# A second expert bias added on TensorE from a resident table, in place of a broadcast transfer a tile

## The chip, the cores and the metric

The kernel runs on one core of one Trainium2 chip. The metric is the device time of one execution in microseconds (us); a lower time is better. The engines are TensorE (PE in the rows; its weight loads are PEld), VectorE (DVE), ScalarE (ACT), GpSimd (POOL) and SyncE (SP), which here only issues transfers. Each engine has an instruction stream of its own and waits on semaphores for the others.

## The reference, cut to what matters

128 images are cut into 64 patches each, projected to 128 numbers (with a class token that makes T = 65 tokens), multiplied by a position table, passed through an LSTM over the tokens, and then through a mixture of 16 experts of which each token uses two. The change is in the last line of the expert step:

```
tokens = einsum('bpi,hi->bph', patches, W) + b ; h = [cls, tokens] * pos_embed
h = h + lstm(layernorm(h))                    # gates = x W_ih' + h W_hh' + biases, 65 steps
xt = layernorm(h)
topk_p, topk_i = top_k(softmax(xt @ router_w.T + router_b), 2)
for each expert e:
    hid = gelu(xt @ w1[e].T + b1[e])           # 128 -> 512
    y   = hid @ w2[e].T + b2[e]                # 512 -> 128, b2[e] is a row of 128
    out += y * gate[e]
h = h + out
```

## The kernel before

There are two stages. In the first, `step(n)` is one time step of the LSTM for all 128 images; beside it the same slot projects the patches of a later token, splits a piece of the expert weights into two fp16 parts, and routes and sends finished tokens to a buffer in HBM that is sorted by expert. In the second, `step_b(n)` works on tiles of 256 sorted rows that belong to one expert each. There are 80 tiles (TILES_B). The order is written out by hand: `slots(step, step_b)` walks both loops for every engine, and each engine executes its part of slot n in the order of the code.

A product of two fp32 matrices is made of three fp16 matmuls (high by high, low by high, high by low), with the weights scaled by E_SCALE = 256. In slot n of the second stage the engines do this:

- **SP** loads the rows of tile n + 3 (`xt`, line L532), after it has waited for `in_ps` and `dst_done` of tile n - 1 (L405). It then waits for `y_done` of tile n - 3, reads the expert number of tile n + 1 into a register (L540) and starts the transfer that spreads row b2[e] over 128 partitions (`b2r`, L542). Loads and stores of finished tokens come behind it in some slots.
- **PE** transposes tile n + 1 (2 fp32 passes, L1408), multiplies tile n by the first weight (12 matmuls over 256 columns, L1434) and tile n - 2 by the second (24 matmuls over 128 columns, L1452). Its waits: `in_done` of an earlier tile before the transposes, `hlo_done` of tile n - 2 ahead of L1434 and again of L1452, and `y_done` of the tile whose PSUM bank is used again.
- **ACT** applies gelu to the four quarters of tile n (L680), then rounds all of it to fp16 (`round_off`, L689). In slots from 54 on it also scales one or two rows of a finished chunk (L669).
- **DVE** casts the input of tile n + 1 (L1107), makes the result `yo` of tile n - 3 out of PSUM (L1114, the line that is changed: result times 1/256 plus `b2r`), makes the low part of the input (L1121), the low part of the hidden layer of tile n - 1 (`remainder`, L1099) and the destination rows (L1132). In slots from 56 on it also adds finished chunks (L1172, L1183).
- **POOL** scatters the two halves of tile n - 3 to HBM (`back`, L1257).

The buffers of the second stage lie in `arena`, the space that `patches` used in the first. Expert numbers of the tiles are read from the table `tabi`.

Of the kernel before, what the change touches and what calls it, by code (L numbers as in the profile page):

```python
# [47 lines left out]
PIECES = E * 2 * FF // PIECE  # L48
TWICE = 16
# [29 lines left out]
C_ID, C_TRI, C_ONE, C_IOTA, C_EBASE, C_TOK, C_BSC, C_POW, C_J = np.cumsum([0, P, P, P, UG * E, E, T, 4, 1]).tolist()  # L79
C_END = C_J + 1  # L80


def constants():

    c = np.zeros((P, C_END), np.float32)
    c[:, C_ID:C_TRI] = np.eye(P)
    c[:, C_TRI:C_ONE] = np.triu(np.ones((P, P)), 1)
    c[:, C_ONE:C_IOTA] = 1.0
    c[:, C_IOTA:C_EBASE] = np.tile(np.arange(E) - E, UG)
    c[:, C_EBASE:C_TOK] = np.arange(E) * CAP  # L90
    c[:, C_TOK:C_BSC] = 2 * (T * np.arange(P)[:, None] + np.arange(T))
    c[:, C_POW] = -0.5
    c[:, C_BSC:C_POW] = [0.5, 0.5, 1.0, 0.5]
    c[:, C_J] = ROWS * np.arange(P)
    return c


def tower(nc, x, w, w_rest, cls, pos, w_ih, w_hh, b_ih, b_hh, rw, rb, we, b1, b2, const, out):
# [3 lines left out]
    with ctx:  # L102
# [71 lines left out]
        h1 = sb("h1", [P, T, HID])  # L174
        ynT = sb("ynT", [HID, 2, B])
# [33 lines left out]
        pad = sb("pad", [P, HALVES, ROW])  # L209

# [14 lines left out]
        b2r = part(4 * HID).rearrange("p (a h) -> p a h", a=4)  # L225
# [77 lines left out]
        b2_in = [sem(f"b2_in{i}") for i in range(4)]  # L303
# [138 lines left out]
        def _(sp):  # L442
            at_row, at_expert, at_pad = (sp.alloc_register(name) for name in ("at_row", "at_expert", "at_pad"))
# [19 lines left out]
            def step(n):  # L463
# [22 lines left out]
                for piece in pieces_of(n + 2):  # L486
                    if piece >= NE:
                        through(sp, ex_lo_done, piece - NE)
                    sp.dma_start(ex_raw[:, piece % NE, :], we[:, bass.ds(piece * PIECE, PIECE)]
                                 ).then_inc(ex_in[piece % NE], 16)  # L490
                if n == 10:
                    sp.wait_ge(setup_dve, 2)
                    sp.dma_start(rows_of(sent, E * CAP), pad[:, :, :]).then_inc(pads, 16)
# [20 lines left out]
            def step_b(n):  # L514
# [18 lines left out]
                j = n + 1  # L533
                if 0 <= j <= TILES_B - 1:
                    if j == 0:
                        sp.wait_ge(tok_done, (T - 1))
                        sp.wait_ge(lo_done, (T - 1))
                    if j >= 4:
                        through(sp, y_done, j - 4)
                    sp.reg_load(at_expert, tabi[0:1, 0, j:j + 1])  # L540
                    e = sp.snap(at_expert, min_val=0, max_val=E - 1)
                    sp.dma_start(b2r[:, j % 4, :],  # L542
                                 b2[bass.ds(e, 1), :].rearrange("a h -> (a h)").partition_broadcast(P)
                                 ).then_inc(b2_in[j % 4], 16)
# [22 lines left out]
        def _(act):  # L567
# [30 lines left out]
            def step(n):  # L598
# [43 lines left out]
                if 0 <= t <= T - 1:  # L642
# [3 lines left out]
                    act.activation(xT_hi[:, t % 2, :], ps_T[:, 0:P], ACT.Copy).then_inc(xT_hi_done, 1)  # L646
                for p in pieces_of(n):
# [66 lines left out]
        def _(dve):  # L714
# [41 lines left out]
            def step(n):  # L756
# [90 lines left out]
                if n > T - 1:  # L847
                    routing(n)
                    rest_of_choice(n)
                if n == PLAN_B:  # L850
# [155 lines left out]
            def plan_piece(k, late):  # L1006
# [8 lines left out]
                start = cst[:, C_J:C_END]  # L1015
# [85 lines left out]
            def step_b(n):  # L1101
# [7 lines left out]
                if 0 <= j <= TILES_B - 1:  # L1109
                    through(dve, down_ps, j)  # L1110
                    dve.wait_ge(b2_in[j % 4], (j // 4 + 1) * 16)
                    if j >= NO:
                        dve.wait_ge(y_out[j % NO], j // NO * 16 * HALVES)
                    dve.scalar_tensor_tensor(yo[j % NO], ps_down(j).rearrange("p (a h) -> p a h", a=HALVES),  # L1114
                                             1.0 / E_SCALE,
                                             b2r[:, j % 4, :].unsqueeze(1).to_broadcast([P, HALVES, HID]), ALU.mult,
                                             ALU.add).then_inc(y_done, 1)
# [146 lines left out]
        def _(pe):  # L1264
# [131 lines left out]
            def step_b(n):  # L1396
# [41 lines left out]
                if 0 <= j <= TILES_B - 1:  # L1438
# [5 lines left out]
                    elif j > 0:  # L1444
                        through(pe, h1_done, T - 1)
                        through(pe, yT_done, T - 1)
                    for c in range(FC):
                        for k, (h_, w_) in enumerate(((hhi, ex_hi), (hlo, ex_hi), (hhi, ex_lo))):
                            w2 = w_[:, bass.ds(e, 1), 1, c * HID:(c + 1) * HID].rearrange("p a f -> p (a f)")
                            for a in range(HALVES):  # L1450
                                h = h_[j % 4][:, c * ROWS + a * P:c * ROWS + (a + 1) * P]
                                last = pe.matmul(ps_down(j)[:, a * HID:(a + 1) * HID], h, w2,  # L1452
                                                 start=(c == 0 and k == 0 and a == 0), stop=(c == FC - 1 and k == 2),
# [47 lines left out]
```

## Time and profile before

| | |
|---|---|
| time, median of 3 runs | 675.24 us (674.0 to 675.88) |
| span of the profiled execution | 771.4 us |
| the profiled execution's own time | not listed apart from its span |
| mean granted TensorE clock | 0.957 of 2.4 GHz |
| busy time PE / DVE / ACT / POOL | 647.2 / 562.3 / 493.0 / 413.1 us |
| first stage (65 LSTM steps) | from 0 to about 410 us of the span |
| tiles: first and last result (L1114) | 426.2 and 753.1 us, 80 of them |

The span runs from the first to the last instruction while every instruction is recorded. The timed runs are made without a recording, and here they are 96 us shorter than the span. A busy share is thus a share of a stretched time, and the time of single instructions and the distance of two that follow each other at once are better guides than shares. A busy matmul time includes the time to drain, during which the next already runs.

### The profile page before, as it was taken

What the parts mean: (1) busy time and instruction counts of PE and PEld (TensorE: products, weight loads), DVE (VectorE), ACT (ScalarE), POOL (GpSimd) and SP (SyncE); (2) the same over time, 40 slices, a digit from 0 to 9 for tenths busy, and PEclk for the clock granted to TensorE, in tenths of its full rate; (3) what the DMA queues carried; (4) which work ended last, traced back from release to release, by engine and by line L of the source; (5) the groups of instructions that cost most, each with busy time, mean ns of one, the idle gap of its engine ahead of it and who ended that gap; (6) DMA issues with size and microseconds to landing.
All of it is one profiled execution on the core that took longest, in us unless ns stands there. A gap on an engine that the chain in (4) does not pass through costs nothing.

```text
span 771.4 us, 24553 instructions
## 1 busy us (share of the span) xinstructions
PE 647.2 (84%) x7952; PEld 594.7 (77%) x7952; DVE 562.3 (73%) x1797; ACT 493.0 (64%) x1259; POOL 413.1 (54%) x446
## 2 busy tenths in 40 slices
PE   4999999999999999988877665878888787888870
PEld 4999999999999999888875554766666666666660
DVE  3877888888888888778886444756565756677777
ACT  4678876766667666554446343657666767777783
POOL 0243344777767666655656646545555555545552
PEclk9999999999999999999997767999999999999995
DMA  8987877888888887765522222344323234444555
GB/s 318 372 263 271 277 253 251 261 267 256 276 261 267 276 244 236 236 213 182 162 64 60 71 63 73 108 123 119 111 78 98 78 93 118 138 137 131 170 177 195
DMA packets 71895, 141.67 MB, mean 184 GB/s; under 512 B 13078, under 2 KB 55650, under 8 KB 63838
## 3 DMA queue, kind: packets, MB, share of 16 engines
q1 hardware_dynamic: 62128, 121.69, 50.1%
q0 software_dynamic: 9280, 17.21, 6.4%
q8 instruction: 70, 1.15, 0.6%
q10 hardware_dynamic: 366, 1.21, 0.5%
q14 instruction: 51, 0.42, 0.2%
HBM read 116.35 MB, written 25.66 MB: 184 GB/s over the span
## 4 chain that ended last, share of the span: by engine, by line
PE 25%; DVE 24%; another core or an unknown queue 13%; issue 13%; ACT 4%; POOL 3%; DMA 1%; POOLq 0%; ACTq 0%; DVEq 0%; SPq 0%
PE pair L1279 14%; DVE patches L1099 7%; PE pair L1434 3%; DVE patches L1121 2%; PE pair L1325 2%; POOL sent L1235 2%; ACT pair L680 2%; PE pair L1452 2%; PE pair L1289 1%; DVE patches L1114 1%; DVE h L1172 1%; DVE patches L1107 1%; DVE patches L1132 1%; DVE field L843 1%
## 5 line engine op out<-in xcount | busy, mean ns | idle before, releaser
L1257 POOL DMA_INDIRECT back<-patches x160 | 157.0, 981 | 150.6 <-DVE patches L1114 104.6
L680 ACT ACTIVATE pair<-pair,b1s 128x256 f32<-128x256 f32 x320 | 126.3, 448 | 110.4 <-remote 51.5
L1279 PE MATMUL pair<-field,patches 128*128 128x128 f32 (+1 forms) x1408 | 173.9, 280 | 8.9 <-DMA patches<-in_x 8.6
L1279 PEld LDWEIGHTS pair<-field,patches 128*128 128x128 f32 (+1 forms) x1408 | 164.6, 194 | 9.6 <-issue 8.6
L1235 POOL DMA_INDIRECT sent<-pay,slot_own x130 | 149.2, 1148 | 40.3 <-issue 38.2
L1434 PE MATMUL pair<-patches,ex_hi 128*128 128x256 f16 x640 | 119.4, 280 | 47.8 <-DVE patches L1099 23.8
L605 ACT ACTIVATE gate<-pair,lbias 128x128 f32<-128x128 f32 x260 | 74.4, 369 | 98.1 <-PE pair L1294 88.6
L1452 PE MATMUL pair<-ex_hi,patches 128*128 x1280 | 117.4, 225 | 8.3 <-issue 6.1
L1247 POOL TENSOR_TENSOR rstd<-veps,cst 128x2 f32<-128x2 f32 (+1 forms) x68 | 58.0, 853 | 107.2 <-DVE veps L800 106.6
L1107 DVE CAST patches<-pair 128x256 f16<-128x256 f32 x80 | 33.7, 422 | 109.6 <-remote 105.2
L1434 PEld LDWEIGHTS pair<-patches,ex_hi 128*128 x640 | 56.6, 99 | 72.8 <-issue 64.0
L1099 DVE TENSOR_TENSOR patches<-pair,patches 128x1024 f16<-128x1024 f32 x80 | 97.5, 1219 | 5.6 <-ACT patches L689 4.7
L1434 PE MATMUL pair<-patches,ex_lo 128*128 128x256 f16 x320 | 89.2, 279 | 13.6 <-issue 13.5
L1452 PEld LDWEIGHTS pair<-ex_hi,patches 128*128 128x128 f16 x1280 | 90.1, 101 | 13.5 <-issue 9.7
L1279 PE MATMUL pair<-field 128*128 128x128 f16 x1536 | 96.1, 219 | 0.0
L1279 PEld LDWEIGHTS pair<-field 128*128 128x128 f16 x1536 | 91.8, 98 | 0.8
L1452 PE MATMUL pair<-ex_lo,patches 128*128 x640 | 90.8, 225 | 0.0
L587 ACT ACTIVATE field<-patches 128x512 f16<-128x512 f32 x128 | 80.9, 634 | 4.6 <-DMA patches<-in_x 4.6
L689 ACT ACTIVATE patches<-pair 128x1024 f16<-128x1024 f32 x80 | 82.0, 1025 | 2.5
L843 DVE TENSOR_TENSOR field<-patches,field 128x1024 f16<-128x1024 f32 x64 | 78.1, 1221 | 0.1
L1209 POOL TENSOR_TENSOR ex_lo<-field,ex_hi 128x256 f16<-128x256 f32 x64 | 45.5, 720 | 43.3 <-ACT field L653 42.6
L1434 PEld LDWEIGHTS pair<-patches,ex_lo 128*128 x320 | 31.9, 100 | 28.0 <-issue 23.6
(150 smaller groups left out, 1257.7 us busy)
## 6 DMA issues: line engine op xcount, KB each, us to landing
patches<-in_x SPq DMA_DIRECT2D x62, 1152.0 KB
patches<-sent SPq DMA_DIRECT2D x80, 130.0 KB
field<-in_we SPq DMA_DIRECT2D x64, 128.0 KB
field<-back SPq DMA_DIRECT2D x10, 768.0 KB
patches<-in_b SPq DMA_DIRECT2D x80, 64.0 KB
field<-in_pos SPq DMA_DIRECT2D x65, 64.0 KB
out_tower<-h SPq DMA_DIRECT2D x10, 384.0 KB
back<-patches POOLq DMA_INDIRECT x160
```

The lines of the kernel that those rows point to most:

```text
L587: return act.activation(xhi[r][:, a:b, :], xraw[q][:, a:b, :], ACT.Copy)
L605: last = act.activation(gate[:, GATE_AT[g], :], ps_gate[n % 2][:, g * B:(g + 1) * B], ACT.Tanh, bias=lbias[:, 2, g:g + 1], scale=(1.0 if g ...
L680: last = act.activation(up[:, cols], up[:, cols], ACT.Gelu, bias=b1s[:, bass.ds(e * FC + 2 * half + i, 1)], scale=1.0 / E_SCALE)
L689: act.activation(hhi[n % 4], pair[n % 2][:, :], ACT.Copy).then_inc(hhi_done, 1)
L843: dve.tensor_tensor(xlo[r][:, :, :], xraw[q][:, 0:KS, :], xhi[r][:, :, :], ALU.subtract).then_inc(lo_done, 1)
L1099: dve.tensor_tensor(hlo[n % 4], pair[n % 2][:, :], hhi[n % 4], ALU.subtract).then_inc(hlo_done, 1)
L1235: pool.indirect_dma_start(sent, bass.IndirectOffsetOnAxis(ap=slot_own[:, g % 4, choice, col:col + 1], axis=0), pay[:, t % NP, :], None, bo ...
L1247: pool.tensor_tensor(rstd[:, both], veps[:, both], cst[:, C_POW:C_POW + 1].to_broadcast([P, both.stop - both.start]), ALU.pow).then_inc(rs ...
L1257: pool.indirect_dma_start(back, bass.IndirectOffsetOnAxis(ap=dsti[j % NO][:, k:k + 1], axis=0), yo[j % NO][:, k, :], None, bounds_check=2 ...
L1279: last = pe.matmul(bank_of, l, w_, start=(c == KS and k == 0), stop=(c == KS - 1 and k == 2))
L1434: last = pe.matmul(ps_up(n, half)[:, i * ROWS:(i + 1) * ROWS], w1, r, start=(k == 0), stop=(k == 2))
L1452: last = pe.matmul(ps_down(j)[:, a * HID:(a + 1) * HID], h, w2, start=(c == 0 and k == 0 and a == 0), stop=(c == FC - 1 and k == 2), skip_ ...
```

## The change

The table of 16 second biases is loaded once, twice over (partitions 0 to 15 and 16 to 31), in slot 0 of the first stage. ACT multiplies it by 256 in slot 4; DVE in slot 5 rounds it to fp16 (`b2_hi`) and forms `b2_parts`: partitions 0 to 15 hold the scaled table rounded to fp16, partitions 16 to 31 hold what the rounding left. The sum of row e and row 16 + e is the bias to about twice the precision of fp16. `chosen` holds two 16 by 16 unit matrices, one above the other. For every tile PE takes column e of it, repeated 128 times, as the stationary operand (32 rows by 128 columns) and `b2_parts` as the moving one, once for each half of the tile. These two matmuls open the accumulation in PSUM that the 24 of L1452 opened before. DVE's L1114 loses its second tensor and becomes a multiplication by a constant. SP loses the register load, the transfer and the wait for `y_done`. The constants `cst` grow by 17 columns. In the diff the name ahead of the point tells the engine (`sp`, `act`, `dve`, `pe`).

```diff
+BIASES_AT = 4
...
+    c[E:2 * E, C_PART] = -1.0
+    c[0:2 * E, C_SEL:] = np.tile(np.eye(E), (2, 1))
...
+        b2_raw = h1[0:2 * E, T - 1, :]
+        b2_hi = h1[0:2 * E, T - 2, 0:HID // 2].bitcast(F16)
...
+        b2_parts = sb("b2_parts", [2 * E, HID], F16)
+        chosen = sb("chosen", [2 * E, E], F16)
...
-        b2r = part(4 * HID).rearrange("p (a h) -> p a h", a=4)
...
+                if n == 0:
+                    for k in range(2):
+                        sp.dma_start(b2_raw[k * E:(k + 1) * E, :], b2).then_inc(b2_in, 16)
...
-                j = n + 1
-                if 0 <= j <= TILES_B - 1:
-                    if j == 0:
-                        sp.wait_ge(tok_done, (T - 1))
-                        sp.wait_ge(lo_done, (T - 1))
-                    if j >= 4:
-                        through(sp, y_done, j - 4)
-                    sp.reg_load(at_expert, tabi[0:1, 0, j:j + 1])
-                    e = sp.snap(at_expert, min_val=0, max_val=E - 1)
-                    sp.dma_start(b2r[:, j % 4, :],
-                                 b2[bass.ds(e, 1), :].rearrange("a h -> (a h)").partition_broadcast(P)
-                                 ).then_inc(b2_in[j % 4], 16)
...
+                if n == BIASES_AT:
+                    act.wait_ge(b2_in, 32)
+                    act.activation(b2_raw, b2_raw, ACT.Copy, scale=E_SCALE).then_inc(b2_scaled, 1)
...
+                if n == BIASES_AT + 1:
+                    dve.wait_ge(b2_scaled, 1)
+                    dve.tensor_copy(b2_hi, b2_raw).then_inc(b2_rounded, 1)
+                    dve.tensor_copy(chosen[:, :], cst[0:2 * E, C_SEL:C_END])
+                    dve.wait_ge(b2_rounded, 1)
+                    dve.scalar_tensor_tensor(b2_parts[:, :], b2_hi, cst[0:2 * E, C_PART:C_PART + 1],
+                                             b2_raw, ALU.mult, ALU.add).then_inc(b2_done, 1)
...
                     through(dve, down_ps, j)
-                    dve.wait_ge(b2_in[j % 4], (j // 4 + 1) * 16)
...
-                    dve.scalar_tensor_tensor(yo[j % NO], ps_down(j).rearrange("p (a h) -> p a h", a=HALVES),
-                                             1.0 / E_SCALE,
-                                             b2r[:, j % 4, :].unsqueeze(1).to_broadcast([P, HALVES, HID]), ALU.mult,
-                                             ALU.add).then_inc(y_done, 1)
+                    dve.tensor_scalar(yo[j % NO], ps_down(j).rearrange("p (a h) -> p a h", a=HALVES), 1.0 / E_SCALE,
+                                      None, ALU.mult).then_inc(y_done, 1)
...
+                    if j == 0:
+                        pe.wait_ge(b2_done, 1)
+                    one = chosen[:, bass.ds(e, 1)].to_broadcast([2 * E, P])
+                    for a in range(HALVES):
+                        pe.matmul(ps_down(j)[:, a * HID:(a + 1) * HID], one, b2_parts[:, :], start=(a == 0),
+                                  stop=False, skip_group_check=True)
                     for c in range(FC):
...
-                                                 start=(c == 0 and k == 0 and a == 0), stop=(c == FC - 1 and k == 2),
+                                                 start=False, stop=(c == FC - 1 and k == 2),
```

PE's instructions of one tile in the middle of the second stage, from the end of the first weight's matmuls to the next tile's transposes, before (ISA and REGISTER_ALU compute addresses from the expert number in a register):

```order
L1434 MATMUL pair<-patches,ex_lo 128x256
L1452 ISA [waits y_done,hlo_done]
L1452 MATMUL pair<-ex_hi,patches 128x128 x4
L1452 REGISTER_ALU
L1452 MATMUL pair<-ex_lo,patches 128x128 x2
```

and at the same place in the changed kernel (its L1439 and L1463 are L1434 and L1452 of before):

```order
L1439 MATMUL pair<-patches,ex_lo 128x256
L1456 ISA [waits y_done,hlo_done]
L1456 MATMUL pair<-b_parts,chosen 128x128 x2
L1463 ISA
L1463 MATMUL pair<-ex_hi,patches 128x128 x4
L1463 REGISTER_ALU
L1463 MATMUL pair<-ex_lo,patches 128x128 x2
```

Two matmuls and one address computation come in behind the wait for `hlo_done`, ahead of the 24 matmuls; the wait itself stays where it was.

SP's instructions of one slot of the second stage, before:

```order
L530 TENSOR_LOAD tabi [waits dst_done,in_ps]
L531 ISA
L532 DMA patches<-sent 128x260
L540 TENSOR_LOAD tabi [waits y_done]
L541 ISA
L542 DMA patches<-in_b 128x128
```

and in the changed kernel, where L540 to L542 are the load of tile rows that was L530 to L532:

```order
L540 TENSOR_LOAD tabi [waits dst_done,in_ps]
L541 ISA
L542 DMA patches<-sent 128x260
```

The second half of the slot's work is gone, with the wait for `y_done`.

## Rows read from the trace of the kernel before

**Rows 1.** The page: span, engine busy times, TensorE clock in 40 slices
```profile
span 771.4 us, 24553 instructions
...
PE 647.2 (84%) x7952; PEld 594.7 (77%) x7952; DVE 562.3 (73%) x1797; ACT 493.0 (64%) x1259; POOL 413.1 (54%) x446
...
PEclk9999999999999999999997767999999999999995
```

**Rows 2.** Busy time by stretch: engine busy us (instructions), clock, DMA share, GB/s
```profile
core 0: us, PE busy (x) PEld busy (x) DVE busy (x) ACT busy (x) POOL busy (x), PEclk, DMA share, GB/s
40.00:120.00 80.00, 80.00 (x1055) 79.64 (x1053) 65.43 (x238) 63.11 (x194) 30.30 (x42) 1.00 0.80 268
410.00:480.00 70.00, 44.96 (x401) 34.87 (x401) 35.00 (x106) 31.81 (x65) 41.43 (x47) 0.76 0.25 70
500.00:640.00 140.00, 113.82 (x1378) 95.05 (x1377) 87.01 (x187) 93.29 (x182) 70.55 (x73) 1.00 0.35 99
660.00:740.00 80.00, 65.30 (x792) 54.42 (x790) 59.00 (x140) 63.26 (x136) 41.21 (x42) 1.00 0.48 146
```

**Rows 3.** Chain that ended last, shares of 20-400 us, then of 440-740 us
```profile
by line: PE pair L1279 28.1%; issue 8.9%; PE pair L1325 4.4%; POOL sent L1235 3.8%; PE pair L1289 3.0%; DVE field L843 2.1%; another core or an unknown queue 2.0%; PE pair L1294 1.5%; POOL rstd L1247 1.2%; PE pair L1380 1.2%; PE pair L1351 
...
by line: another core or an unknown queue 27.9%; issue 17.8%; DVE patches L1099 17.4%; PE pair L1434 6.8%; DVE patches L1121 5.7%; ACT pair L680 4.2%; PE pair L1452 3.6%; DVE patches L1114 2.9%; DVE patches L1107 2.7%; DVE patches L1132 2.5
```

**Rows 4.** Timeline of PE in one tile: start, us, instruction
```profile
600.08 0.39 PE L1434 MATMUL pair<-patches,ex_hi 128*128 128x256 f16 x2 [0.61 <-DVE patches L1099]
...
601.29 0.27 PE L1434 MATMUL pair<-patches,ex_lo 128*128 128x256 f16 x1
601.40 0.39 PE L1452 MATMUL pair<-ex_hi,patches 128*128 x4
601.62 0.28 PE L1452 MATMUL pair<-ex_lo,patches 128*128 x2
...
602.63 0.28 PE L1452 MATMUL pair<-ex_lo,patches 128*128 x2
602.74 0.39 PE L1408 MATMUL pair<-cst,patches 128*128 128x128 f32 x2
602.97 0.38 PE L1434 MATMUL pair<-patches,ex_hi 128*128 128x256 f16 x2
```

**Rows 5.** Timeline of all engines just after, 603.0 to 605.6 us
```profile
603.05 0.97 POOL L1257 DMA_INDIRECT back<-patches  x1 [0.30 <-issue]
...
603.62 0.27 PE L1434 MATMUL pair<-patches,ex_hi 128*128 128x256 f16 x1
...
604.99 0.27 PE L1434 MATMUL pair<-patches,ex_hi 128*128 128x256 f16 x1 [1.09 <-issue]
...
605.32 0.42 DVE L1107 CAST patches<-pair 128x256 f16<-128x256 f32 x1 [2.13 <-remote]
...
605.49 0.45 ACT L680 ACTIVATE pair<-pair,b1s 128x256 f32<-128x256 f32 x1 [1.44 <-remote]
```

**Rows 6.** Who waited for whom, whole span, then the DMA queue's own waits
```profile
POOL back L1257 <- DVE patches L1114: 104.6, 40, 4.0
...
PE pair L1434 <- DVE patches L1099: 23.8, 36, 1.4
...
PE pair L1408 <- DVE patches L1121: 2.8, 1, 2.8
...
SPq L540 <- DVE patches L1114: 71.8, 40, 7.6
```

**Rows 7.** Groups by line, 660 to 740 us: busy us, mean ns
```profile
L669 ACT ACTIVATE field<-field,gates 128x128 f32<-128x128 f32 x31 | 11.0, 392 | 0.0
...
L1114 DVE SCALAR_TENSOR_TENSOR patches<-pair,patches 128x256 f32<-128x256 f32 x21 | 8.8, 417 | 0.0
...
L1107 DVE CAST patches<-pair 128x256 f16<-128x256 f32 x20 | 8.5, 423 | 19.6 <-remote 18.8 <-PE pair L1408 0.7
```

**Rows 8.** Line L1279, the projection's weight loads: ns min/median/max, forms
```profile
L1279 PEld LDWEIGHTS pair<-field,patches x1408: 186/192/333, 7.9 to 396.0; 128*128 128x128 f32 x160, 65*128 65x128 f32 x16
```

More of the change, by code:

```diff
@@ L76 @@
 NO = 12
-C_ID, C_TRI, C_ONE, C_IOTA, C_EBASE, C_TOK, C_BSC, C_POW, C_J = np.cumsum([0, P, P, P, UG * E, E, T, 4, 1]).tolist()
-C_END = C_J + 1
+C_ID, C_TRI, C_ONE, C_IOTA, C_EBASE, C_TOK, C_BSC, C_POW, C_J, C_PART, C_SEL = np.cumsum(
+    [0, P, P, P, UG * E, E, T, 4, 1, 1, 1]).tolist()
+C_END = C_SEL + E
 def constants():
@@ L302, in tower @@
         xt_in = [sem(f"xt_in{i}") for i in range(4)]
-        b2_in = [sem(f"b2_in{i}") for i in range(4)]
+        b2_in, b2_scaled, b2_rounded, b2_done = sem("b2_in"), sem("b2_scaled"), sem("b2_rounded"), sem("b2_done")
         in_ps, in_hi, in_done = sem("in_ps"), sem("in_hi"), sem("in_done")
@@ L442, in _ @@
         def _(sp):
-            at_row, at_expert, at_pad = (sp.alloc_register(name) for name in ("at_row", "at_expert", "at_pad"))
+            at_row, at_pad = (sp.alloc_register(name) for name in ("at_row", "at_pad"))
             def load_patches(t):
@@ L1014, in plan_piece @@
                 took = [taken[:, i * E:(i + 1) * E] for i in range(2)]
-                start = cst[:, C_J:C_END]
+                start = cst[:, C_J:C_J + 1]
                 def prefix(rounds):
```

## The prediction

> **What bounds the kernel now.** I first asked which of the two stages the change can touch, then what paces a tile there. The page gives busy shares of the whole span [rows 1]; since the span of the profiled execution (771.4 us) is 96 us longer than the median of the timed runs (675.24 us), I looked for what stretched it. The chain that ended last has a share that nothing in the profile releases, "another core or an unknown queue": 2.0% of the 380 us of the first stage, but 27.9% of the 300 us from 440 on [rows 3]. That is 7.6 + 83.7 = 91 us, close to the 96. One such piece is visible by the instruction: PE is in the middle of a run of matmuls at 603.62, the next one starts at 604.99, and DVE and ACT start again at 605.32 and 605.49 after waits on "remote", while POOL, which issues few instructions, was at work at 603.05 [rows 5]. What DVE waited for (transposes at 602.74) was long done [rows 4]. I take these stops as the price of the recording, and they recur about once in two tiles. They are not in the 675 us. So the sum below is made on distances between instructions in pieces without a stop, and added to 675.24; the profiled execution's own span says little about the change.
>
> Second stage, one tile of PE [rows 4]: the 12 matmuls of L1434 run from 600.08 to 601.40 (0.110 each), the 24 of L1452 from 601.40 to 602.74 (0.056 each), the two transposes from 602.74 to 602.97 (0.115 each). Sum 2.89 us, with no gap in it, and the next tile follows at once. The other engines by busy time and tile: there are 38 matmuls a tile, so from 500 to 640 us (1378 matmuls) there are 36.3 tiles [rows 2], 3.86 us each with the stops. ACT has 93.29 / 36.3 = 2.57 us, DVE 87.01 / 36.3 = 2.40, POOL 1.94 plus an issue of 0.3 before each of its two scatters = 2.5. If 27.9% of 3.86 us is the recording, 2.78 are left, about PE's 2.89. Therefore in the timed runs I expect PE to pace the tiles at about 2.9 us from about tile 11 on. The waits agree: POOL waits for DVE 104.6 us in all, while PE waits only 23.8 us for `remainder` (L1099) [rows 6], in a trace in which the stops hold DVE back.
>
> From 660 to 740 us (792 matmuls, 20.8 tiles) the merging of finished tokens adds ACT's L669, 31 times 392 ns [rows 7]: ACT has 63.26 / 20.8 = 3.04 us a tile, DVE 2.83 [rows 2]. Busy times overlap at their ends, so ACT's true pace is less than that. There PE and ACT are about equal.
>
> **The change part by part.**
>
> *Two matmuls a tile on PE.* No row shows this form (32 rows, a repeated column as weights). Nearest rows: fp16, 128 columns, 0.056 us from start to start, and the fp32 passes with the same 128 columns, whose loads are slower, 0.115 [rows 4]. I take the first, since operand type, columns and PSUM writes are the same; 0.115 is the upper bound. That only 32 rows are filled I count as no saving: among the 1408 fp32 loads of L1279 there are some with 65 rows, and the shortest of all took 186 ns against a median of 192 [rows 8]. So 2 x 0.056 = 0.112 us a tile, 80 tiles: 9.0 us of PE work (upper bound 18.4). Below, no gain is possible here, since it is added work. The Trainium skill, "TensorE: Matmul & The Clock Gate", section "LDWEIGHTS (loading the stationary operand)", says that a load takes time by its columns and not by its rows; rows 8 agree. The same page, section "Back-to-back issue gap", gives some 81 ns as the sustained spacing of matmuls with 128 columns in streams with weight loads; the trace has 56 for just such a stream, and the measurement decides. By the page the added work would be an estimated 13 us.
>
> *One address computation.* It stands behind the wait for `hlo_done` but goes through the sequencer while L1434's matmuls still run; the address instructions that a tile has now leave no gap in rows 4. I cost it at nothing; without the cover it is below one spacing, 0.05 us a tile, 4 us.
>
> *What of the 9.0 us shows.* The matmuls stand in PE's order ahead of the next transposes and of L1434, so where PE paces the tiles they show in full. (a) Tiles 11 to 53: PE paces, 43 x 0.112 = 4.8 us. (b) Tiles 54 to 79: ACT is nearly as slow as PE; I let two thirds show: 26 x 0.112 x 2/3 = 1.9 us. (c) Tiles 0 to 10, during the end of the LSTM and the routing: from 410 to 480 us PE is busy 44.96 of 70 us and the clock is at half its level in part (mean 0.76) [rows 2]; the tiles wait for others, but the work also costs more at the lower clock. I let half show: 11 x 0.112 / 2 = 0.6. (d) The last tile lies on the end of the chain; the clock falls in the last slices [rows 1]: 0.1. Sum 7.4 us.
>
> *DVE's L1114.* It takes 417 ns with two tensors, and L1107, which reads one tensor of the same size from PSUM, takes 423 [rows 7]. The second operand costs nothing, so its removal gives nothing. If it gave a third (0.14 us a tile), DVE has 0.4 us a tile of room anyway and nobody would gain. The wait for `b2_in` never ends last in the waits that I read.
>
> *SP.* The slot loses a register load, one issue and the wait for `y_done`, on which SP spent 71.8 us [rows 6]. That wait ended in DVE's slot n; the next thing in SP's queue waits for `dst_done` of tile n, which is later in the same slot. So tile rows are loaded when they were before. PE's transposes waited once, 2.8 us, and that was for DVE [rows 6]; I found no wait of theirs for a transfer. The DMA share is 0.35 to 0.48 in the second stage [rows 2], so 64 KB less a tile frees nothing that was short. 0.
>
> *Setup.* One operation on ACT (32 x 128) and three on DVE, at most 0.42 us each by the larger L1107, in slots 4 and 5 of the first stage, plus two small transfers. There PE is busy without a gap (80.00 of 80 us), DVE 65.43, ACT 63.11 [rows 2]: hidden. Without that cover 1.5 us. The wait for the table stands four slots behind its transfer.
>
> Forecast: 675.24 + 7.4 = 682.6 us. I say **682.5**.
>
> **The rivals.**
>
> *Hidden (same).* If in the timed runs a loop through ACT and DVE paces the tiles (weights' first product, gelu, rounding, `remainder`, and back to PE), PE has room and 0.112 us fits in it. For it: the unrecorded pace can't be read directly, and ACT's 2.57 is only 0.3 below PE. Against: PE's run of 2.89 us has no gap, and by it `remainder` of the last tile was done before the next L1434 wanted it at 602.97. Then only (c) and (d) show: 676 us.
>
> *Dear.* The form loads slowly (0.115) and the address computation shows: 0.23 to 0.28 us a tile, over the 80 tiles less the hidden part (factor 7.4 / 9.0): +15 to +18 us, 690 to 693 us.
>
> *Faster.* The removed transfer matters: without the stops of the recording tiles follow in 2.9 us instead of 3.86, so the load of `xt` has a quarter less time. If it came too late, PE would wait for it in each tile, and SP's second issue and its wait, gone now, would free about 0.3 us a tile. It decides from the point where transposes wait more than 0.11 us a tile for `xt`. 60 tiles x 0.3 = 18 less, plus 7.4: 665 us. Against: loads run two slots ahead, and no wait of this kind is in the rows.
>
> **How the numbers follow.** What can be told from no change on this kernel is about 0.3%, 2.0 us: the three runs lie within 1.9. Chances: forecast 0.63 (its own range 679 to 686), hidden 0.17, dear 0.12, faster 0.08. Slower is forecast plus dear, 0.75; same is 0.17; faster 0.08. The range goes from the hidden case to the lower edge of the dear one: 676 to 689.5; outside stay the faster case, most of the dear one and the lower half of the hidden one.
>
> **What would show it.** In the new profile the two matmuls stand between L1434 and L1452's successors with 0.056 from start to start and the tile's run on PE is 3.00 us; the DVE line has a mean of 415 to 425; POOL still waits for DVE. PE's waits for `remainder` should shrink. The span itself need not grow, since it is set by the stops: PE's records rise by five a tile and SP's fall by as many. The forecast is wrong if the new matmuls are spaced at 0.1 or more, or if the timed median stays under 677, which would mean that PE has room.

## The result and the profile after

The changed kernel takes 687.29 us (median of 4 runs, 686.49 to 687.57); the kernel before has 674.62 us beside it (4 runs). The ratio is 1.0189, with an interval of 1.016 to 1.0217: slower by 12.7 us. The forecast was 682.5 with a range of 676 to 689.5. Two later runs of the kernel before, 906.58 and 1612.11 us beside 25 that lie from 670.98 to 677.62, are left out of the ratios below.

The page of the changed kernel: span, busy times, TensorE clock, and the chain that ended last by engine and by line:

```profile
span 685.3 us, 24627 instructions
...
PE 639.8 (93%) x8112; PEld 596.3 (87%) x8112; DVE 563.7 (82%) x1800; ACT 491.6 (72%) x1260; POOL 415.4 (61%) x446
...
PEclk9999999999999999999999989999999999999995
...
PE 63%; DVE 7%; issue 4%; ACT 3%; POOL 2%; DMA 1%; POOLq 0%; ACTq 0%; SPq 0%; DVEq 0%
PE pair L1284 22%; PE pair L1463 14%; PE pair L1439 12%; PE pair L1330 4%; PE pair L1294 3%; PE pair L1413 2%; PE pair L1456 2%; DVE patches L1107 2%; PE pair L1299 1%; PE pair L1385 1%; ACT pair L681 1%; DMA field<-back 1%; POOL sent L1240 1%; PE pair L1319 1%; PE pair L1356 1%
```

The span is 685.3 us, 2 below the timed runs, where the first trace of before had 771.4 [rows 1]. The stops are gone: the share "another core or an unknown queue" of [rows 3] is not in this chain at all, and 63% of the chain is PE. In the changed kernel L1439 is L1434 of before, L1463 is L1452, L1456 the two new matmuls, L1413 the transposes, L1107 `remainder`, L1121 the result line, L1115 the input cast.

PE in one tile of the changed kernel (timeline: start, us, instruction):

```profile
560.17 0.38 PE L1439 MATMUL pair<-patches,ex_hi 128*128 128x256 f16 x2
...
561.38 0.27 PE L1439 MATMUL pair<-patches,ex_lo 128*128 128x256 f16 x1
561.58 0.28 PE L1456 MATMUL pair<-b_parts,chosen 32*128 32x128 f16 x2
561.79 0.40 PE L1463 MATMUL pair<-ex_hi,patches 128*128 x4
...
563.14 0.39 PE L1413 MATMUL pair<-cst,patches 128*128 128x128 f32 x2
563.37 0.38 PE L1439 MATMUL pair<-patches,ex_hi 128*128 128x256 f16 x2
```

The answer to [rows 4]. L1439's own matmuls are spaced as L1434's were, but the first short matmul comes 0.20 us after the last long one (561.38 to 561.58) where 0.11 was due, and the first of L1463 comes 0.21 us after the pair began, where 0.11 was due. The 24 matmuls of L1463 take 1.35 us instead of 1.34. From L1439 to L1439 it is 3.20 us, against 2.89 in [rows 4]: the two matmuls cost 0.31 us a tile, not 0.112.

Busy time by stretch (the columns of [rows 2]) of the changed kernel:

```profile
450.00:570.00 120.00, 119.83 (x1499) 103.11 (x1497) 89.81 (x199) 95.85 (x186) 81.21 (x85) 1.00 0.36 104
575.00:645.00 70.00, 70.00 (x878) 60.22 (x876) 60.48 (x141) 63.67 (x137) 42.60 (x44) 1.00 0.48 149
```

A tile has 40 matmuls now, so in 120 us there are 37.5 tiles, 3.20 us each, and 3.19 in the later stretch. PE has no idle time to speak of. Two waits of the changed kernel:

```profile
DVE patches L1115 <- PE pair L1413: 43.1, 66, 1.0
POOL back L1262 <- DVE patches L1121: 42.0, 45, 1.8
```

DVE waits for PE all along, and POOL for the result line behind it; in this trace the transposes never wait for a load of tile rows. Of the signs that the prediction named, two came, POOL's wait and an unchanged time of the result line (a mean of 0.414 us); the third, 3.00 us a tile, did not.

### The profile page after: what moved, and what is told of

Read it like the earlier page. It is cut to its first block, busy times and chain, and to the rows that moved or that the text cites. A ratio compares the mean times of both kernels' runs of the same rounds, so it can differ in the third digit from the quotient of the medians.

```text
span 685.3 us, 24627 instructions
## 1 busy us (share of the span) xinstructions
PE 639.8 (93%) x8112; PEld 596.3 (87%) x8112; DVE 563.7 (82%) x1800; ACT 491.6 (72%) x1260; POOL 415.4 (61%) x446
## 4 chain that ended last, share of the span: by engine, by line
PE 63%; DVE 7%; issue 4%; ACT 3%; POOL 2%; DMA 1%; POOLq 0%; ACTq 0%; SPq 0%; DVEq 0%
PE pair L1284 22%; PE pair L1463 14%; PE pair L1439 12%; PE pair L1330 4%; PE pair L1294 3%; PE pair L1413 2%; PE pair L1456 2%; DVE patches L1107 2%; PE pair L1299 1%; PE pair L1385 1%; ACT pair L681 1%; DMA field<-back 1%; POOL sent L1240 1%; PE pair L1319 1%; PE pair L1356 1%
## 5 line engine op out<-in xcount | busy, mean ns | idle before, releaser
L1240 POOL DMA_INDIRECT sent<-pay,slot_own x130 | 151.5, 1165 | 39.7 <-issue 36.9
L681 ACT ACTIVATE pair<-pair,b1s 128x256 f32<-128x256 f32 x320 | 123.6, 448 | 38.9 <-PE pair L1439 38.7
L1439 PE MATMUL pair<-patches,ex_hi 128*128 128x256 f16 x640 | 110.4, 274 | 2.8 <-DVE patches L1107 2.2
L1463 PE MATMUL pair<-ex_hi,patches 128*128 x1280 | 112.2, 220 | 0.0
L1107 DVE TENSOR_TENSOR patches<-pair,patches 128x1024 f16<-128x1024 f32 x80 | 97.0, 1213 | 0.9 <-ACT patches L690 0.8
L1463 PEld LDWEIGHTS pair<-ex_hi,patches 128*128 128x128 f16 x1280 | 81.8, 98 | 8.3
L1463 PE MATMUL pair<-ex_lo,patches 128*128 x640 | 87.9, 219 | 0.0
L1439 PE MATMUL pair<-patches,ex_lo 128*128 128x256 f16 x320 | 87.8, 274 | 0.0
L1439 PEld LDWEIGHTS pair<-patches,ex_hi 128*128 x640 | 61.8, 98 | 11.3 <-issue 4.3
L1115 DVE CAST patches<-pair 128x256 f16<-128x256 f32 x80 | 33.9, 423 | 44.1 <-PE pair L1413 43.1
L1330 PE MATMUL pair<-xT_hi,wih_hi 128*128 128x128 f16 x260 | 47.8, 221 | 2.6 <-DVE xT_lo L761 2.6
```

The lines of the kernel that those rows point to most:

```text
L681: last = act.activation(up[:, cols], up[:, cols], ACT.Gelu, bias=b1s[:, bass.ds(e * FC + 2 * half + i, 1)], scale=1.0 / E_SCALE)
L1107: dve.tensor_tensor(hlo[n % 4], pair[n % 2][:, :], hhi[n % 4], ALU.subtract).then_inc(hlo_done, 1)
L1240: pool.indirect_dma_start(sent, bass.IndirectOffsetOnAxis(ap=slot_own[:, g % 4, choice, col:col + 1], axis=0), pay[:, t % NP, :], None, bo ...
L1330: pe.matmul(ps_gate[t % 2][:, g * B:(g + 1) * B], w_[:, g, :], r[:, t % 2, :], start=(g == 0 and k == 0), stop=False, skip_group_check=True)
L1439: last = pe.matmul(ps_up(n, half)[:, i * ROWS:(i + 1) * ROWS], w1, r, start=(k == 0), stop=(k == 2))
```

## Experiments

The runs of one group share the runs of before next to them; ratios are to those.

### A second trace of the kernel before

> The unchanged kernel of before, for a second trace. Both theories: 674.6 us. If the stops of the first trace were the recording's, they need not come again; then the span is about 672 us and a tile takes 3.0 us (3.20 of after less 12.7 us over 69 tiles), not PE's 2.89 of instruction distances, so PE would idle about 0.1 us a tile. If PE paces the tiles as the prediction had it, PE has no gap and a tile takes 2.89; then after's 0.31 us a tile should have cost 20 us and more, and the missing 8 us must have been gained elsewhere.

No edit. One timed run of 674.1 us, 673.1 for the others. The page, same parts:

```profile
span 672.3 us, 24553 instructions
...
PE 620.9 (92%) x7952; PEld 588.8 (88%) x7952; DVE 562.0 (84%) x1797; ACT 489.7 (73%) x1259; POOL 412.6 (61%) x446
...
PEclk9999999999999999999999989999999999999895
...
PE 59%; DVE 8%; issue 5%; DMA 4%; POOL 3%; ACT 1%; POOLq 0%; SPq 0%; ACTq 0%; DVEq 0%
```

The span is 672.3 us. The same kernel had 771.4 in its first trace, while its timed runs agree (674.62 and 673.1 us), so the 99 us between them were the first recording's, as the prediction took them. What stopped the engines there, no trace shows. PE in one tile, in the second trace:

```profile
520.95 0.39 PE L1452 MATMUL pair<-ex_hi,patches 128*128 x4
...
522.29 0.39 PE L1408 MATMUL pair<-cst,patches 128*128 128x128 f32 x2
522.63 0.39 PE L1434 MATMUL pair<-patches,ex_hi 128*128 128x256 f16 x2
```

The 24 matmuls of L1452 take 1.34 us (520.95 to 522.29), as in [rows 4]. But from the first transpose to the first long matmul there are 0.34 us (522.29 to 522.63) where [rows 4] have 0.23. Over the tiles from 455 to 560 us the step from the second transpose to the long matmul has a median of 0.179 us where matmuls that follow at once have 0.109. So PE did idle in before, by about 0.07 us a tile (its busy time does not show it, since the ends of matmuls are modelled). The stretches show it (1553 matmuls by 38 are 40.9 tiles, 2.94 us each) and something else in the later one:

```profile
450.00:570.00 120.00, 119.88 (x1553) 108.42 (x1551) 97.67 (x213) 104.63 (x205) 87.25 (x91) 1.00 0.49 140
575.00:645.00 70.00, 66.89 (x831) 59.13 (x829) 62.55 (x148) 63.96 (x141) 42.67 (x45) 0.98 0.57 173
```

Here 831 / 38 = 21.9 tiles in 70 us are 3.20 us each, as slow as the changed kernel, and the clock is not at its higher level all the time. The waits between 560 and 650 us, and one of them in the timeline of PE:

```profile
PEld pair L1408 <- DMA patches<-sent: 3.0, 3, 1.8
...
PE pair L1408 <- DMA patches<-sent: 2.4, 2, 1.6
```

```profile
600.41 0.44 PE L1408 MATMUL pair<-cst,patches 128*128 128x128 f32 x2 [0.79 <-DMA patches<-sent]
601.07 0.39 PE L1434 MATMUL pair<-patches,ex_hi 128*128 128x256 f16 x2 [0.21 <-issue]
```

The transposes of one tile wait until 600.41 for tile rows. SP's issues before that:

```profile
592.30 0.58 SPq L542 DMA_DIRECT2D patches<-in_b  x1
592.93 0.43 SPq L506 DMA_DIRECT2D field<-back  x1
593.94 0.33 SPq L532 DMA_DIRECT2D patches<-sent  x1
```

Behind a bias transfer (L542) and the 768 KB of finished tokens (L506), the rows of this tile were asked for at 593.94 and were there 6.4 us later; with nothing ahead such a load takes 2 to 3 us. In all, PE's weight loads waited 3.0 us for rows, in three tiles (0.3, 1.0 and 1.8 us).

The longest of these waits cost more than itself. It ended at 629.01 (PE had started nothing since 627.2), and from 629.7 to 633.1 us the granted clock was at 1.2 GHz, the lower of its two levels:

```profile
629.66 0.58 PE L1434 MATMUL pair<-patches,ex_hi 128*128 128x256 f16 x2 [0.21 <-issue]
630.25 0.63 PE L1434 MATMUL pair<-patches,ex_hi 128*128 128x256 f16 x2
630.68 0.42 PE L1434 MATMUL pair<-patches,ex_lo 128*128 128x256 f16 x1
```

Two matmuls of L1434 take 0.43 us there (630.25 to 630.68) instead of 0.22, and the tile's 36 matmuls 4.32 us instead of 2.65, which is 1.7 us lost on top of the wait. Behind the shorter wait until 600.41 the clock did not fall. The run with unread transfers below shows the same (a wait of 3.1 us, then the lower level from 631.0 to 634.4); the changed kernel's clock stays up through this stretch.

This is the rival that the prediction gave 8 in 100, in a small form.

Where the 13.0 us between the spans of the two kernels lie, by the starts of `remainder`: 1.9 us are there at the first tile (404.1 and 405.9), ahead of every bias matmul; up to the 12th tile 1.0 more (442.6 and 445.5), from there to the 54th 9.9 (567.9 and 580.7), from there to the 80th -0.1 (650.0 and 662.7), and behind it 0.3. The 1.9 us at the first tile are no price of the matmuls: over this case's traces other than the stretched one that start lies anywhere from 404.1 to 407.1 us, in kernels with and without them. From the first `remainder` to the 12th, the six traces without bias matmuls have 38.6 to 38.7 us, those with two (or one wide one) 39.1 to 39.6, the one with four 40.2.

### The change without its matmuls

```diff
-                    one = chosen[:, bass.ds(e, 1)].to_broadcast([2 * E, P])
-                    for a in range(HALVES):
-                        pe.matmul(ps_down(j)[:, a * HID:(a + 1) * HID], one, b2_parts[:, :], start=(a == 0),
-                                  stop=False, skip_group_check=True)
...
-                                                 start=False, stop=(c == FC - 1 and k == 2),
+                                                 start=(c == 0 and k == 0 and a == 0), stop=(c == FC - 1 and k == 2),
```

> The changed kernel without its two bias matmuls a tile: the second bias is left out of the result, the transfers are gone. It parts the price of the matmuls from what the removed transfer and the lighter VectorE line give. If the removal gives nothing (the prediction): 674.6 plus or minus 1, a tile takes what it takes in before. If the removal gives something that hid part of the cost of the matmuls: 666 to 670 us.

670.45 us, ratio 0.9962 (0.9948 to 0.9976). The removed transfers and the lighter DVE line are worth 2.6 us, so the matmuls cost about 15: 1.0189 / 0.9962 = 1.0228. Up to the 54th tile this kernel keeps step with before (569.0 against 567.9 us); the gain is made behind it (646.9 against 650.0 at the last tile). The transposes waited for rows once, 0.5 us.

### What makes the two matmuls dear

Rows filled up to 128 with zeros:

```diff
-        b2_parts = sb("b2_parts", [2 * E, HID], F16)
-        chosen = sb("chosen", [2 * E, E], F16)
+        b2_parts = sb("b2_parts", [P, HID], F16)
+        chosen = sb("chosen", [P, E], F16)
...
+                dve.memset(b2_parts[:, :], 0.0).then_inc(b2_clear, 1)
...
-                    dve.tensor_copy(chosen[:, :], cst[0:2 * E, C_SEL:C_END])
+                    dve.tensor_copy(chosen[:, :], cst[:, C_SEL:C_END])
...
-                    one = chosen[:, bass.ds(e, 1)].to_broadcast([2 * E, P])
+                    one = chosen[:, bass.ds(e, 1)].to_broadcast([P, P])
```

> The changed kernel with both operands of the bias matmuls filled up with zeros to 128 rows; the repeated column stays. Theory rows (the change from 128 rows to 32 and back costs about 0.1 us each time, since loads and matmuls don't overlap over it): a tile takes 3.00 instead of 3.20 us, about 675 to 679 us in all. Theory column (a repeated column loads slowly) and theory address (the address computation shows): no change, 687 us.

679.54 us, ratio 1.0088 (1.0059 to 1.0117). PE in one tile of this kernel:

```profile
560.11 0.39 PE L1441 MATMUL pair<-patches,ex_hi 128*128 128x256 f16 x2
...
561.32 0.27 PE L1441 MATMUL pair<-patches,ex_lo 128*128 128x256 f16 x1
561.43 0.28 PE L1458 MATMUL pair<-b_parts,chosen 128*128 128x128 f16 x2
561.54 0.39 PE L1465 MATMUL pair<-ex_hi,patches 128*128 x4
...
562.88 0.39 PE L1415 MATMUL pair<-cst,patches 128*128 128x128 f32 x2
563.12 0.39 PE L1441 MATMUL pair<-patches,ex_hi 128*128 128x256 f16 x2
```

The short matmuls start 0.11 us after the last long one and 0.11 ahead of L1465: no loss on either side, 0.056 each. So of the 0.31 us, 0.2 came from the rows. Not all of it is gained: a tile takes 3.01 in this piece but 3.08 at the median, 0.12 less than in the changed kernel, since PE idles 0.08 us behind the transposes again (0.19 us from the second transpose to the long matmul, at the median, where the changed kernel has 0.109).

Contiguous weights at a fixed address, still 32 rows:

```diff
-                    one = chosen[:, bass.ds(e, 1)].to_broadcast([2 * E, P])
+                    one = ones16[0:2 * E, :]
```

> The changed kernel with the first 32 rows of the resident fp16 ones as the stationary operand in place of the repeated column: contiguous weights, a fixed address, still 32 rows; each row gets the sum of all 16 biases instead of its own. Theory rows: no change, 687 us and 3.20 us a tile. Theories column and address: the 0.2 us beyond two normal matmuls go away, 3.00 us a tile, 675 to 679 us.

685.15 us, ratio 1.0181 (1.015 to 1.0212), which is the changed kernel's within the interval. Its timeline of PE has the same two steps of 0.20 and 0.22 us:

```profile
559.80 0.27 PE L1439 MATMUL pair<-patches,ex_lo 128*128 128x256 f16 x1
560.00 0.28 PE L1456 MATMUL pair<-b_parts,ones 32*128 32x128 f16 x2
560.22 0.40 PE L1463 MATMUL pair<-ex_hi,patches 128*128 x4
```

So neither the repeated column nor the address computation of the bias matmuls costs anything that can be told.

Four short matmuls instead of two:

```diff
-                    for a in range(HALVES):
-                        pe.matmul(ps_down(j)[:, a * HID:(a + 1) * HID], one, b2_parts[:, :], start=(a == 0),
-                                  stop=False, skip_group_check=True)
+                    for i in range(2):
+                        for a in range(HALVES):
+                            pe.matmul(ps_down(j)[:, a * HID:(a + 1) * HID], one, b2_parts[:, :],
+                                      start=(i == 0 and a == 0), stop=False, skip_group_check=True)
```

> The changed kernel with four 32-row matmuls a tile instead of two, the two of them issued twice (the second bias is added twice). Theory rows says that the price is paid once for going to 32 rows and once for coming back, about 0.2 us, and each matmul costs 0.056 to 0.067: a tile takes 3.20 + 0.12 = 3.32 us, the whole 687 + 9 = 696 us. If instead each short matmul by itself costs 0.155 us (0.31 / 2): 3.51 us a tile, 711 us.

694.06 us, ratio 1.0305 (1.0269 to 1.0342), 3.31 us a tile. The timeline of PE:

```profile
521.19 0.27 PE L1439 MATMUL pair<-patches,ex_lo 128*128 128x256 f16 x1
521.39 0.39 PE L1457 MATMUL pair<-b_parts,chosen 32*128 32x128 f16 x4
521.72 0.40 PE L1464 MATMUL pair<-ex_hi,patches 128*128 x4
```

Again 0.20 us into the group; the group of four takes 0.33. Two more matmuls cost 0.11 us, the price of two normal ones. The other 0.2 are paid once a group: for the change of form, not for the matmuls.

64 rows, the other 64 left out (on the kernel with full rows):

```diff
-                    one = chosen[:, bass.ds(e, 1)].to_broadcast([P, P])
+                    one = chosen[0:P // 2, bass.ds(e, 1)].to_broadcast([P // 2, P])
...
-                        pe.matmul(ps_down(j)[:, a * HID:(a + 1) * HID], one, b2_parts[:, :], start=(a == 0),
+                        pe.matmul(ps_down(j)[:, a * HID:(a + 1) * HID], one, b2_parts[0:P // 2, :], start=(a == 0),
```

> The run with full rows, but both operands of the bias matmuls taken from the first 64 partitions. Theory 'any matmul on fewer than all rows pays the change': 3.20 us a tile and about 686 us, as with 32 rows. Theory 'only the 32-row form pays': 3.07 to 3.08 us a tile, 679 us, as with 128 rows.

686.5 us, ratio 1.0177 (1.0125 to 1.023), 3.20 us a tile. PE:

```profile
563.29 0.27 PE L1441 MATMUL pair<-patches,ex_lo 128*128 128x256 f16 x1
563.50 0.28 PE L1458 MATMUL pair<-b_parts,chosen 64*128 64x128 f16 x2
563.71 0.40 PE L1465 MATMUL pair<-ex_hi,patches 128*128 x4
```

64 rows pay like 32. The 65-row matmuls of L1279 in the first stage (fp32) are not among those that pay: they follow their 128-row neighbours at 0.11 us in the trace, as 128-row fp32 ones do. No run has fp16 matmuls on 65 to 127 rows. The Trainium skill, "TensorEngine Tiling (Array Packing)", section "Key Properties", says that a change of the array's tiling mode drains the engine, and its section "When to Use Tiling" names contractions over up to 64 rows as the case for row tiles. The runs fit this, if a matmul on 32 or 64 rows is such a mode by itself: 32 and 64 rows pay about 0.1 us each way, 128 don't. That the time is a drain is argued from the page; no trace here shows what the array does in it.

### What the transfers cost

Transfers and waits as in before, DVE's line as in the changed kernel:

```diff
-                    dve.scalar_tensor_tensor(yo[j % NO], ps_down(j).rearrange("p (a h) -> p a h", a=HALVES),
-                                             1.0 / E_SCALE,
-                                             b2r[:, j % 4, :].unsqueeze(1).to_broadcast([P, HALVES, HID]), ALU.mult,
-                                             ALU.add).then_inc(y_done, 1)
+                    dve.tensor_scalar(yo[j % NO], ps_down(j).rearrange("p (a h) -> p a h", a=HALVES), 1.0 / E_SCALE,
+                                      None, ALU.mult).then_inc(y_done, 1)
```

> The kernel before with the transfers and their waits kept, but VectorE's line made the single-tensor multiplication of the changed kernel, so the second bias is left out of the result. Its counterpart is the kernel without bias and without transfers (0.996 of before). Theory transfer traffic: what that one gained comes from the removed transfers, which delay the loads of tile rows; then this one is as before, 673 us. Theory VectorE line: the gain came from the lighter line, then 670.5 us.

674.6 us, ratio 1.0004 (0.9982 to 1.0025): DVE's line is worth nothing that can be told. Then the same with 512 B a transfer:

```diff
-                    sp.dma_start(b2r[:, j % 4, :],
-                                 b2[bass.ds(e, 1), :].rearrange("a h -> (a h)").partition_broadcast(P)
-                                 ).then_inc(b2_in[j % 4], 16)
+                    sp.dma_start(b2r[0:1, j % 4, :], b2[bass.ds(e, 1), :]).then_inc(b2_in[j % 4], 16)
```

> As the run with unread transfers, but each of the 80 transfers brings the row to one partition (512 B) in place of 128 (64 KB), so issue, register load and waits on SyncE stay and the bytes go; the second bias is left out of the result. Theory bytes: 670.5 us, and the load of the rows of tile 61 lands about 2.5 us after its issue instead of 5.4. Theory SyncE's queue (its issue and its wait for y_done): 673 us.

671.53 us, ratio 0.9957 (0.9936 to 0.9979), as without any transfer. It is the traffic of 80 x 64 KB that costs (bytes and packets go together here and are not told apart), not SP's issues and waits. The rows of tile 61 landed 3.8 us after their issue, not 2.5 as expected and as in the kernel without transfers; the 768 KB are ahead of them in both, but with SP's other work kept they are asked for 1.85 us behind that load, without it 2.55. The transposes waited for rows once, 1.1 us.

The loads of finished tokens in two halves, one slot apart (`LOADS` is the table of their slots), on the kernel before, bias transfers kept:

```diff
-                sp.dma_start(bk[m % NB][:, 0:2 * size, :], back.rearrange("(b r) h -> b r h", r=2 * T)
-                             [:, 2 * t:2 * (t + size), :]).then_inc(bk_in[m % NB], 16)
+                for half in halves:
+                    a, z = ((0, CHUNK // 2), (CHUNK // 2, size))[half]
+                    sp.dma_start(bk[m % NB][:, 2 * a:2 * z, :], back.rearrange("(b r) h -> b r h", r=2 * T)
+                                 [:, 2 * (t + a):2 * (t + z), :]).then_inc(bk_in[m % NB], 16)
...
-                    load_back(LOADS[n])
+                    load_back(LOADS[n], (0,))
+                if n - 1 in LOADS:
+                    load_back(LOADS[n - 1], (1,))
```

The waits for these loads on ACT and DVE (not in the diff above) count 32 a load in place of 16.

> The kernel before with its bias transfers, and the loads of finished tokens (768 KB) that stand between the tiles issued as two halves in two slots. Theory transfer traffic: the loads of tile rows are late since they queue behind 768 KB and the bias transfers; with half of it ahead of them they land in time, three waits of about 1.3 us go: 669 to 671 us, like the kernel without transfers. If only the bias transfers' own packets matter: no change, 673.

672.12 us beside 673.99, ratio 0.9968 (0.9945 to 0.999). In its trace no transposes wait for rows, and the clock stays at the higher level in this stretch. It is the one version here that computes everything and beats both kernels.

### Where PE's 0.07 us of idling in before comes from

PE's register load for the next tile's expert stands between the two halves of the first weight's matmuls, instead of at the head of the tile:

```diff
-                    pe.reg_load(expert[n % 4], tabi[0:1, 0, n:n + 1])
+                    if n in (0, EARLY):
+                        pe.reg_load(expert[n % 4], tabi[0:1, 0, n:n + 1])
...
+                        if half == 0 and n + 1 <= TILES_B - 1 and n + 1 != EARLY:
+                            pe.reg_load(expert[(n + 1) % 4], tabi[0:1, 0, n + 1:n + 2])
```

> The kernel before with one line moved: PE reads the expert number of tile n + 1 in the middle of tile n's first product, instead of between the transposes and the first product of tile n + 1. In the second trace of before the first matmul of a tile comes 0.18 us after the last transpose instead of 0.11. Theory register load: it is the 0.3 us load there that the queue doesn't cover; a tile takes 2.89 instead of 2.96 us, 673 - 4 = 669 us. Theory front end: the issue of instructions as a whole is the limit, wherever the load stands; no change.

675.27 us, ratio 1.0029 (1.001 to 1.0048). PE:

```profile
520.73 0.39 PE L1408 MATMUL pair<-cst,patches 128*128 128x128 f32 x2
520.95 0.38 PE L1435 MATMUL pair<-patches,ex_hi 128*128 128x256 f16 x2
...
521.50 0.27 PE L1435 MATMUL pair<-patches,ex_lo 128*128 128x256 f16 x1
521.69 0.39 PE L1435 MATMUL pair<-patches,ex_hi 128*128 128x256 f16 x2
...
522.24 0.27 PE L1435 MATMUL pair<-patches,ex_lo 128*128 128x256 f16 x1
522.37 0.40 PE L1455 MATMUL pair<-ex_hi,patches 128*128 x4
```

The step behind the transposes is 0.22 for two, as it should be, but the gap has moved: 0.19 us at the new place of the load (521.50 to 521.69) and 0.13 ahead of L1455. Nothing is gained, the kernel is even a little slower. The theory that the idling would go if the load stood elsewhere falls.

One matmul of 256 columns over full rows instead of two of 128:

```diff
-                    for a in range(HALVES):
-                        pe.matmul(ps_down(j)[:, a * HID:(a + 1) * HID], one, b2_parts[:, :], start=(a == 0),
-                                  stop=False, skip_group_check=True)
+                    pe.matmul(ps_down(j).rearrange("p (a h) -> p a h", a=HALVES), one,
+                              b2_parts[:, :].unsqueeze(1).to_broadcast([P, HALVES, HID]), start=True,
+                              stop=False, skip_group_check=True)
```

> The changed kernel with zeros up to 128 rows and both halves of the tile in one matmul over 256 columns (the 128 columns of the table read twice). It costs 0.109 us on PE like the two of 128 columns, but one load, one matmul less to issue. If the array sets the pace: a tile takes 3.07 as with full rows, 679 us. If the issue of instructions sets it (theory front end): 3.00, 674 to 676 us.

678.24 us, ratio 1.0052 (1.0034 to 1.0069). The rows around the transposes and around the new matmul:

```profile
560.92 0.39 PE L1415 MATMUL pair<-cst,patches 128*128 128x128 f32 x2
561.24 0.39 PE L1441 MATMUL pair<-patches,ex_hi 128*128 128x256 f16 x2
...
562.44 0.27 PE L1441 MATMUL pair<-patches,ex_lo 128*128 128x256 f16 x1
562.55 0.27 PE L1457 MATMUL pair<-b_parts,chosen 128*128 128x256 f16 x1
562.66 0.39 PE L1465 MATMUL pair<-ex_hi,patches 128*128 x4
```

The wide matmul costs 0.11 us, like two narrow ones, and the idling behind the transposes is still there (0.32 us for two, 0.23 without a gap); a tile has 3.07 us. Fewer instructions to issue did not shorten it. With the split loads added:

> As the one wide matmul, with the split loads as well. The bias transfers are gone, and PE is a little slower, so that loads of rows are in time nearly everywhere already; one late load (tile 75) could be saved: 1 us less than the run with the one wide matmul alone, at most.

678.54 us, ratio 1.0053 (1.0032 to 1.0073): no difference, as the transposes of neither waited for rows.

## Why the prediction was right, and where its sizes were off

**Direction, bound and range.** Slower, 687.3 inside 676 to 689.5, by the mechanism that had 0.63: PE paces the tiles and the two matmuls add to its work. The profile after shows it in every tile. The time lies above that case's own range of 679 to 686, and below the dear case's 690 to 693, though a tile's price was above that case's too.

**Luck in the number.** Two terms were wrong in opposite directions. The matmuls cost about 15 us and not 7.4, and the removed transfers gave back 2.6 and not 0. With the true price and the prediction's nothing for the transfers the sum would be 675.24 + 15 = 690, just outside the range.

**The stops of the recording** were read rightly: 91 us by the chain, 99 us between two traces of one kernel. Taking durations from pieces without a stop gave 2.89 us a tile, against a median of 2.95 in an unstretched trace.

**Term "two matmuls a tile", 0.112 us: mis-sized.** It measured 0.31 in the tile. The step that failed was to take the spacing of matmuls of the same kind for matmuls of another form. 0.112 is right with 128 rows (shown by the full rows) and for every further short one (shown by the four); the group pays 0.1 us going to 32 rows and 0.1 coming back (shown by 32 against 128 rows, by 64 rows, by contiguous weights). "That only 32 rows are filled I count as no saving" was true and looked only for a gain. The upper bound, 0.115 a matmul, was too low as well, since it was sought among loads and not at the borders between forms.

**"What of it shows".** (a) For tiles 11 to 53, 4.8 us were forecast and 9.9 measured: 0.31 less the 0.07 that PE idled in before and no longer does, is 0.24 us, by 42 tiles from the 12th to the 54th. The idling was not seen in [rows 4], one tile of a stretched trace. (b) For tiles 54 to 79, 1.9 us were forecast and nothing is left of it (-0.1), but not since ACT hid it: against the kernel without matmuls (77.9 us from the 54th to the 80th tile, the changed one 82.0) the price shows there too, 4.1 us or 0.16 a tile. It is offset by what went with the transfers: 3.0 us of waits for rows became 0.5, and the 1.7 us at the lower clock are gone. (c) For the first 11 tiles, 0.6 was forecast and 1.0 measured from the first to the 12th, 0.1 a tile; the other 1.9 us of the difference at the 12th are spread of the first stage. (d) 0.1 against 0.3.

**SP and the transfers, 0: wrong by 2.6 us.** The rival "faster" gave the right mechanism (rows late without the stops of the recording) and the wrong place: not each tile but those behind a 768 KB load. It also put the gain on SP's issue and wait, where it is the traffic. No wait of this kind was in the stretched trace, where tiles took 3.86 us, so the row that was missing was taken for an absence.

**DVE's line and setup, 0:** right. Ratio 1.0004 with the line alone; at the 12th tile the kernel without matmuls is 0.5 us behind before (443.1 and 442.6), within the spread of 404.1 to 407.1 us that the first stage has over the traces.

**What stays open** is why PE idles 0.07 us behind the transposes. It follows the register load when that is moved, does not shrink with fewer matmuls, and is gone where the array loses 0.2 us anyway. The traces show that PE's sequencer has little lead there: its register load takes 0.30 us and starts 0.38 us ahead of the first transpose in the kernel before, 0.35 with full rows, but 0.82 in the changed kernel, where nothing idles (medians from 455 to 560 us). Which of the sequencer's instructions would have to go for the lead to suffice is not shown.

## What to carry to other kernels

A few matmuls on 64 rows or less inside a stream of full ones cost the change of form on top of their columns: fill the operands with zeros to full height (here 679.5 us in place of 687.3, half of the slowdown), or put all of the small form together. Before a transfer is called hidden, look at what it stands behind and ahead of in the queue, and at a trace whose pace is that of the timed runs. If a span is much longer than the timed runs, take a second trace before waits that are absent are used as evidence.

## What the runs showed of the hardware

- A change between 128-row fp16 matmuls and 32- or 64-row ones on TensorE costs about 0.1 us each way (from 455 to 560 us 0.205 us instead of 0.109 going in, 0.147 instead of 0.056 coming back, medians), at the clock's higher level. With weights that repeat one column and with contiguous ones the kernel takes the same time (ratios 1.0189 and 1.0181).
- One kernel's trace can be 15% longer than its run (771.4 against 672.3 us for another trace of it), with 91 us of the chain in stops that hold PE, ACT and DVE at once and have no cause in the trace ([rows 3], [rows 5]).
- A 130 KB load of rows takes 2 to 3 us alone and up to 6.4 us behind a 768 KB load and a 64 KB transfer, at a mean DMA share of only 0.57 (575 to 645 us, second trace of before).
- After PE had waited 1.8 us for rows, the granted clock was at 1.2 GHz from 629.7 to 633.1 us and the tile took 1.7 us longer; behind a wait of 1.0 us it stayed at 2.4 GHz.
